# Identity products ahead of waits of TensorE in a four-layer kernel of attention and experts

## The reference

```python
x = x + L0_xattn(layernorm(x), ctx)      # 16 heads, a mask is added
x = x + L0_attn(layernorm(x))            # 16 heads, softmax with clip and 1e-6, 1e-8 terms
x = x + L0_ffn(layernorm(x))             # 8 experts of 1024, two for each token, and a shared one
x = x + L1_xattn(layernorm(x), ctx)      # 8 heads of 64, both sides normalised
x = x + L1_attn(layernorm(x))            # a gated recurrence over the 64 steps, 32 heads
x = x + L1_ffn(layernorm(x))             # 4 small experts, two for each token
x = x + L2_xattn(...); L2_attn(...)      # 2 transformer layers; L2_ffn: 8 experts, one for each token
x = x + L3_xattn(...); L3_attn(...)      # one transformer layer with rotary positions
x = x + L3_ffn(layernorm(x))             # 32 experts of 2048, each takes the best 8 of 64 tokens
```

## Time and profile before

| | us |
|---|---|
| median of 3 runs | 3578.55 (3578.19 to 3585.3) |
| profiled execution, first to last instruction | 3577.8 |
| TensorE busy | 3140.3 (88%) |
| VectorE busy | 1190.4 (33%) |
| ScalarE busy | 695.5 (19%) |
| mean granted TensorE clock | 0.933 |

### The profile page before, as it was taken

One profiled execution on the slowest core, in us unless ns is written; L12 is line 12 of the kernel. 1 busy time (PEld: TensorE's weight loads), 2 busy tenths in 40 slices (PEclk: granted clock), 3 DMA queues, 4 the chain that ended last, 5 costly groups with the idle time before them and its releaser, 6 DMA issues. The chain is left out here.

```text
span 3577.8 us, 41207 instructions
## 1 busy us (share of the span) xinstructions
PE 3140.3 (88%) x16833; PEld 1532.5 (43%) x16833; DVE 1190.4 (33%) x2513; ACT 695.5 (19%) x1295; POOL 137.7 (4%) x182
## 2 busy tenths in 40 slices
PE   8998879997899899999899989989998997666666
PEld 4444644343444444344467665434445652111111
DVE  3555430002344569765341132113444411000000
ACT  2443101101233331111012120003342211000000
POOL 1000010001000000001000000000000100000000
PEclk9998879999999999989999999999998998888878
DMA  3101069998211022221530111981001258999999
GB/s 144 44 29 39 13 244 417 413 423 345 88 71 47 27 71 65 101 83 36 222 155 12 67 73 55 418 338 48 25 22 46 111 211 337 420 420 420 420 420 372
DMA packets 102911, 654.11 MB, mean 183 GB/s; under 512 B 19048, under 2 KB 28264, under 8 KB 39784
## 3 DMA queue, kind: packets, MB, share of 16 engines
q1 hardware_dynamic: 98064, 638.19, 44.2%
q0 software_dynamic: 4160, 13.63, 1.0%
q10 hardware_dynamic: 536, 0.14, 0.0%
HBM read 642.41 MB, written 9.50 MB: 182 GB/s over the span
## 5 line engine op out<-in xcount | busy, mean ns | idle before, releaser
L2926 PE MATMUL banks<-ring,h 128*32 128x512 f32 x1024 | 162.7, 746 | 78.8 <-DMA ring<-in_L_ffn_w 53.5
L2909 PE MATMUL banks<-ring,mine 128*32 128x512 f32 x1024 | 161.0, 692 | 60.9 <-DMA ring<-in_L_ffn_w 60.4
L1690 PE MATMUL banks<-ring,xT 128*64 128x512 f32 x736 | 166.0, 605 | 15.0 <-DMA ring<-in_L_ffn_Wu 7.1
L504 PE MATMUL banks<-normed_features,first 128*128 128x256 f32 x768 | 168.0, 379 | 1.1 <-ACT normed_features L471 1.1
L504 PEld LDWEIGHTS banks<-normed_features,first 128*128 128x128 f32 x768 | 144.6, 190 | 23.0 <-issue 3.2
L3037 DVE COPY mine<-mT 128x32 f32<-128x32 f32 x31 | 5.6, 182 | 443.0 <-PE banks L2909 443.0
L807 PE MATMUL banks<-ctxT,wkb 128*128 128x512 f32 x256 | 115.4, 596 | 2.1 <-PEq L142 2.1
L811 PE MATMUL banks<-big 128*128 128x512 f32 x256 | 116.8, 602 | 0.0
L807 PE MATMUL banks<-ring 128*128 128x512 f32 x256 | 115.5, 596 | 1.4 <-PEq L142 1.4
L811 PE MATMUL banks<-ring 128*128 128x512 f32 x256 | 115.6, 596 | 0.0
L811 PE MATMUL banks<-wvb,ctxT 128*128 128x512 f32 x256 | 115.6, 596 | 0.0
(11 more groups left out here) (613 smaller groups left out, 4851.6 us busy)
## 6 DMA issues: line engine op xcount, KB each, us to landing
ring<-in_L_ffn_w SPq DMA_DIRECT2D x256, 1024.0 KB, 27.1
ring<-in_L_ffn_Wd SPq DMA_DIRECT2D x24, 2048.0 KB, 21.0
ring<-in_L_ffn_Wg SPq DMA_DIRECT2D x23, 2048.0 KB, 23.9
ring<-in_L_ffn_Wu SPq DMA_DIRECT2D x23, 2048.0 KB, 20.9
wb<-in_L_ffn_W SPq DMA_DIRECT2D x32, 1024.0 KB, 24.1
first<-in_L_ffn_W SPq DMA_DIRECT2D x16, 1024.0 KB, 19.9
second<-in_L_ffn_W SPq DMA_DIRECT2D x16, 1024.0 KB, 22.0
ctxT<-in_ctxT SPq DMA_DIRECT2D x8, 1024.0 KB, 4.9
```

The lines of the kernel that those rows point to most:

```text
L504: ins = pe.matmul(m.ps[:, self.banks[q % R], 0:256], w[:, k, mm * P:(mm + 1) * P], m.yT[:, k, 256 * half:256 * half + 256], start=(k == 0) ...
L1690: ins = pe.matmul(ps[H * side:H * side + H, 2 * kind + half, :], xT[:, p % 2, k, H * own:H * own + H], rows_of(where[(name, slot)], C)[:, ...
L2909: ins = pe.matmul(ps[B4 * q:B4 * q + B4, 0, :], mine[:, e % 2, k, :], w[:, q * 512:(q + 1) * 512], start=(k == 0), stop=(k == C - 1))
L2926: ins = pe.matmul(ps[B4 * q:B4 * q + B4, 2, :], h[:, Q * n + q, :], w[:, q * D:(q + 1) * D], start=(n == 0), stop=(n == Q - 1))
```

## The change

A helper `run_idle(m, pe, bank, n)` is added. It multiplies the 128 x 128 identity by itself n times into a bank that nothing reads between, with no semaphore. It is called at 16 places on TensorE, 506 products in all. In `turn_output` the wait for `added` moves ahead of them, and the wait for `normed` stays behind. At three places a wait that guards the bank is added ahead of them (`v_taken`, `taken`, `z_taken`).

```diff
@@ -146,6 +146,13 @@
             yield b
+def run_idle(m, pe, bank, n):
+    for _ in range(n):
+        pe.matmul(m.ps[:, bank, 0:P], m.ident[:], m.ident[:], start=True, stop=True)
@@ -258,6 +265,7 @@
             def _(pe):
+                run_idle(m, pe, 4, 20)
                 for c in range(C):
@@ -580,6 +588,7 @@
             else:
+                run_idle(m, pe, 6, 14)
                 pe.wait_ge(*norm.taken.at(C))
@@ -640,6 +649,7 @@
         def _(pe):
+            run_idle(m, pe, 7, 20)
             norm.turn(pe, 0)
@@ -857,6 +868,8 @@
             if knorm:
+                if head:
+                    run_idle(m, pe, 6, 26)
                 for c in range(C):
@@ -902,6 +915,9 @@
                         attend(b, par, j // G)
+                    if end and j + 1 < J:
+                        pe.wait_ge(*v_taken.at(KC * B))
+                        run_idle(m, pe, 0, 6)
@@ -1184,9 +1200,10 @@
             def turn_output(t):
-                pe.wait_ge(*normed.at(t + 1))
                 if t:
                     pe.wait_ge(*added.at(t))
+                run_idle(m, pe, 7, ((12, 24, 8, 10) if custom else (8, 16, 0, 0))[t])
+                pe.wait_ge(*normed.at(t + 1))
                 for c in range(C):
@@ -1665,12 +1682,14 @@
+                run_idle(m, pe, 7, 6)
                 pe.wait_ge(*made.at(2))
                         rank()
+                run_idle(m, pe, 7, 30)
                 pe.wait_ge(*hs_ready.at(4))
@@ -1987,6 +2006,8 @@
             multiply(3)
+            pe.wait_ge(*taken.at(T))
+            run_idle(m, pe, 4, 14)
             norm.turn(pe, 0)
@@ -2578,6 +2599,7 @@
             gate(0)
+            run_idle(m, pe, 6, 16)
             norm.turn(pe, 1)
@@ -2723,10 +2745,12 @@
+            run_idle(m, pe, 5, 16)
             pe.wait_ge(*chosen.at(1))
             ins.then_inc(*counted.up())
+            run_idle(m, pe, 5, 8)
             pe.wait_ge(*dispatched.at(1))
@@ -2887,6 +2911,7 @@
             ins.then_inc(*b2_turned.up())
+            run_idle(m, pe, 6, 8)
             pe.wait_ge(*kept_ready.at(1))
@@ -3550,6 +3576,8 @@
                     pe.matmul(ps[:, i, 0:CB], mean[:], one, start=True, stop=True).then_inc(*meaned.up())
+            pe.wait_ge(*z_taken.at(5))
+            run_idle(m, pe, 4, 20)
             pe.wait_ge(out_sent.sem, out_sent.made)
```

## The result

The changed kernel takes 3559.83 us (median of 4 runs, 3548.39 to 3560.51) against 3579.32 (4 runs, 3578.19 to 3585.3) for the kernel before: a ratio of 0.9934, with a 95% interval of 0.992 to 0.9949. Measured again later, beside eight runs of before, it was 3554.73 against 3581.38, ratio 0.9923 (0.9907 to 0.994). The profiled execution spans 3558.8 us, 19.0 less than before's, and the mean granted clock rose from 0.933 to 0.954. The likeliest time of the prediction was 3538; about half of the gain forecast is there.

The account below looks back on a forecast made before the run. The end follows L3_ffn's twenty-first chunk, issued at 2972.01, by a fixed length; ahead of it, serial chains run partly at half clock. Gains and losses by place sum to 41.2 us: 3577.8 to 3536.6, median 3538; range 3518 to 3564.

Parts of the forecast that it names:

- The output tiles of L0: L0's four self-attention output tiles: 54 products fit into 16.1 us of waits and the tiles reach full clock; 8.8 us gained.
- L1's tail: End of L1's cross-attention: waits of 0.28 us are shorter than six products (1.34 us); 1.0 us lost.
- the recurrence's first products: First 20 products, behind the barrier at the recurrence outputs: 7 us of delay, 4.4 us regained behind; -2.6 us.
- rival (b): Whole kernel: the clock falls all the same late in waits or in narrow work; half the gain, 3558 us; chance 0.18.
- the stretch with L0_ffn and L1's cross-attention: From L0's output tiles through L0_ffn to L1's head, second context and tail; 17.6 us gained.
- Last tokens of L2: 16 products in a wait of 5.12 us bring the turn and the gate behind it to full clock; 2.2 us gained.
- L0's head and tail: L0's features at the head gain 0.6 us and the half-clock tail, its waits longer than six products, 3.5; together 4.1.
- L1's output: 14 products before the first turn: delay taken out of the 3.42 us wait between turns, what follows starts warm; +2.0 us.
- L2's self-attentions: Output tiles of L2's two self-attention layers: products fit under waits up to 4.7 us; 8 us gained.
- the recurrence outputs: First 20 products cost 2.6 us net, second 20 gain 1.6 in a wait of 5.80; together -1.0 us.
- (a): Whole kernel: products cost 0.43 us each and outlast their waits, beyond 0.27 to 0.30 is delay; about 3644 us; chance 0.08.
- (c): Whole kernel: DMAs that blocks wait for take the gain back before the end; 3565 to 3578 us; chance 0.06.

Follow-up runs that it names:

- pad_early: The kernel before with 78 products of 4 columns added at the very start, no other change; 3607.58 us, 27 us over before.
- outputs_narrow: The changed kernel with only the products of `turn_output` kept, in the same numbers but 8 columns wide in place of 128; 3595.08 us, ratio to before 1.0033.
- half: The changed kernel with half of the products at each of the 16 places, 253 in all; 3580.06 us, ratio to before 0.9995.
- moved: `waits_only` with products added before the recurrence outputs' barrier, between L1's output turns, in L0's and L3's tails, before last-tile scores in L2 and L3; 3550.97 us, ratio 0.9915.
- best: `moved` plus 20 products in `normalise`, 15 at the heads of L1, L2 and L3, 18 before L2's head; 3548.51 us, ratio to before 0.9906.
- outputs_double: The changed kernel with only the products of `turn_output` kept, in twice the number; 3589.4 us, ratio to before 1.0017.
- waits_only: The changed kernel without products at block heads, tails, L1's output, L2_ffn and the first 20 of the recurrence outputs; 246 stay; 3559.66 us, ratio to before 0.9937.

## Why the prediction was half right

**Right.** The sum of the terms is 3537.4, rounded up to 3538 in the prediction. What bounds the end (596 us from the re-issue, moved as a whole) and that a microsecond ahead of it is a microsecond of the span. The price of a product, 0.224 us and not 0.324, in full waits. The output tiles of L0: 8.8 forecast, 8.1 measured, the fourth at the 5.05 us reckoned; the 0.7 is the idle 0.25 us of a tile, which stays and was taken off for three of them. L1's tail, -1.0 forecast and -0.9 measured, and the recurrence's first products: 7 us of delay forecast, 7.6 measured. The time lies in the range, and is that of rival (b), 3558. That it is so near is luck in part: (b) halves the whole sum, and measured, some terms came whole and others with the wrong sign.

**Right by two errors that cancel: the stretch with L0_ffn and L1's cross-attention, 17.6 forecast, 15.6 measured.** The tiles gave 8.1 (8.8), L0_ffn up to its experts 4.9 (5.8), L1's head 1.2 (1). The 26 products before the second context were to give 3 and gave 0.0: they filled the wait to 1.0 us and the first three turns behind them ran at full clock, but in the waits of 0.87 between these short turns the clock fell, the fourth turn took 1.12 us, and what had been gained was lost in the projections behind it. The 1.9 that make up for it came between there and the tail; `pad_early` and `outputs_narrow`, with no product near, have 2.0 there too.

**Rival (b), and why.** Its mechanism was named: the clock falls in the last part of a wait, or in narrow work. `half`, `outputs_narrow` and the tail show both. Last tokens of L2 are its plain case: 2.2 forecast, 0.7 measured in that block (1.4 in the second execution), since in the changed kernel the gate behind the second turn still took 3.58 us:

```profile
2216.82 1.44 PE L462 MATMUL banks<-identity,normed_tokens 128*128 128x128 f32 x8 [1.44 <-DVE normed_tokens L445]
2219.12 3.58 PE L2591 MATMUL banks<-gw,normed_features 128*128 128x8 f32 x16 [0.86 <-ACT normed_features L479]
```

**Wrong, L0's head and tail: 4.1 forecast, -3.9 measured, the largest miss.** The step that failed was "the waits (2.02 before the turn) are longer than six products". They are, and one of them is 4.78 (shown with the experiment): six left 3.16 of it open, so the half clock stayed and the next six cost 2.93. The tail was to give 3.5 and cost 0.4, with what follows it 0.9; L3's, where the same wait is 3.26, gave 4.3. How much twenty products bring in L0's tail is less sure: `moved` gained 1.8 in it and 2.2 behind it, `best`, with the same products, 1.3 and nothing, since there the clock fell in the last products with v; and `outputs_double`, with none in the tail, has 2.2 behind it. And the head was thought over by its own gain alone. It was 0.8 us earlier at its last product, the next block begins when it did, and TensorE's wait there, 2.14 us in the kernel before (first row), is 2.87:

```profile
31.96 1.10 PE L807 MATMUL banks<-ctxT,wkb 128*128 128x512 f32 x2 [2.14 <-PEq L142]
```

```profile
31.89 1.19 PE L817 MATMUL banks<-ctxT,wkb 128*128 128x512 f32 x1 [2.87 <-PEq L142]
```

Behind it the clock is half until 38.0, where before it was full all through, and 3.0 us are lost. Here the gain that the barrier absorbed lengthened the wait at the barrier. The four profiles with products at L0's head all fell there, behind waits of 2.83 to 4.23 us, and lost 1.5 to 3.0 (1.7 in the second execution of the changed kernel); the eight without them waited 1.39 to 2.14 us and did not fall.

**Wrong, L1's output: 2.0 forecast, -2.0 measured.** "The delay is taken out of that wait nearly whole" was right (3.1 lost, 3.1 back); "what follows starts warm" was wrong, for the barrier behind. From the second turn to the end of the stretch 0.3 was lost in both executions, so the term was worth about 0. The 2.0 that are lost come from a fall of the clock ahead of these products, which `waits_only` has as well, and whose cause stays open.

**Mis-sized, L2's self-attentions: 8 forecast, 3.3 measured in their own two blocks (1846.9 to 1963.8 and 2049.2 to 2165.4), 4.1 in the second execution.** The first gained 3.4. In the second the tiles were 3.6 shorter, and the stop of 2.84 us with the late turn took 3.8; a cost that no row of before could show.

**Mis-sized, the recurrence outputs: -1.0 forecast, -2.9 measured.** Delay 7.6 and not 7; the second 20 products, reckoned at 1.6, gained nothing that can be told from the 4.6 of the block (1.0 in `waits_only`, which has them alone).

**The rivals.** (a) was right in its point and wrong in its price for the waits; 0.38 and 0.49 us for a product were measured only behind an idle stretch (recurrence outputs, second six of L0's tail). (c) holds for two places (L0's head, last tokens with L2_ffn) and not for the kernel. Its 0.08 and 0.06 were fair; 0.18 for (b) was too little: a place by place reckoning takes all waits as covered, and nearly all errors of its terms had one sign (only L3's tail and self-attention gave more than forecast).

## What to carry to other kernels

Products whose result nobody reads may be put into a wait of TensorE if they fill it nearly whole, have the columns of real ones (128 here, where 8 failed), and start right behind the work before. Here the numbers that left up to 1.16 us of a wait open kept the clock in all four tiles of L0 in every profile that had them; half of the number kept it in one of the four and gained nothing in the sum, and double, tried for the output tiles, was a loss. Ahead of a barrier, in the wait for it, they cost nothing here; behind it each was delay at the half-clock price. A number is to be set from the longest wait of each place: the same code had 4.78 us in L0 and 3.26 in L3, and six products failed in one and served in the other. And a sum over places by "busy time at half clock, halved" is an upper bound: take the half only of what the other engines wait for, and look what the gained time does to the next barrier. Last, compare several executions before a fall of the clock is put down to an edit near it.

## What was not expected of the hardware

- Products of 8 columns and of 128 take the same time in a run (24 of them 5.42 and 5.52 us), and only the wide ones leave the clock at 1.00; behind the narrow ones it was 0.62.
- TensorE stopped for 1.6 to 2.8 us within runs of small products, 14 times in eleven profiles. Within a layer's attention the stops of all kernels lie whole multiples of 256 records apart, and TensorE goes on 1.3 to 1.5 us behind a packet of the instruction queue.
- The same list of TensorE does not have its clock fall at the same places. Two executions of the changed kernel differ behind the same wait (3.0 and 1.7 us lost at 31.9 us), `moved` and `best` differ at the end of L0's tail and in L1's output; the runs of the changed kernel range from 3548.39 to 3560.51.
